# Projection of the second attention's last two chunks as entries of its score ring

## The reference

```python
x = x + _layernorm(_L0_attn_ref(_layernorm(x), ...))   # low-rank q and kv, rotary, causal softmax attention
x = x + _layernorm(_L0_ffn_ref(_layernorm(x), ...))    # int8 weights: silu(x Wg) * (x Wu), then Wd
x = x + _layernorm(_L1_attn_ref(_layernorm(x), ...))
x = x + _layernorm(_L1_ffn_ref(_layernorm(x), ...))
```

```python
qkv = jnp.einsum('bsd,ed->bse', x, w_qkv) + b_qkv
scores = jnp.einsum('bhqd,bhkd->bhqk', q, k) / math.sqrt(Hd) + causal
out = jnp.einsum('bhqk,bhkd->bhqd', jax.nn.softmax(scores), v)
return jnp.einsum('bsd,ed->bse', out, w_out) + b_out
```

## Time and profile before

| | us |
|---|---|
| median of 3 runs (1263.5 to 1268.62) | 1264.33 |
| profiled execution | 1264.68 |
| its span, first to last instruction | 1262.9 |
| TensorE busy | 1159.9 (92%) |
| VectorE busy | 1051.2 (83%) |
| ScalarE busy | 730.6 (58%) |
| GpSimd busy | 334.6 (26%) |

### The profile page before, as it was taken

One profiled execution on the slowest core, in us unless ns is written; L12 is line 12 of the kernel. 1 busy time (PEld: TensorE's weight loads), 2 busy tenths in 40 slices (PEclk: granted clock), 3 DMA queues, 4 the chain that ended last, 5 costly groups with the idle time before them and its releaser, 6 DMA issues.

```text
span 1262.9 us, 35540 instructions
## 1 busy us (share of the span) xinstructions
PE 1159.9 (92%) x14872; PEld 588.7 (47%) x14872; DVE 1051.2 (83%) x2746; ACT 730.6 (58%) x925; POOL 334.6 (26%) x561
## 2 busy tenths in 40 slices
PE   5779999999999998799997799999999999987996
PEld 4432344544444543565653324455444444454664
DVE  6869999999999863887776799999999988558776
ACT  2441377767677887244452507777767788843332
POOL 2321211122111223434342312111131112424443
PEclk9976699999999999899997759999999999998999
DMA  5263000211200000001123420021120000000001
GB/s 175 90 205 102 21 15 15 65 28 30 50 4 2 3 3 3 1 34 37 51 64 102 113 78 15 15 58 28 29 57 4 3 3 3 4 1 1 17 18 34
DMA packets 31600, 49.95 MB, mean 40 GB/s; under 512 B 7245, under 2 KB 24143, under 8 KB 31431
## 3 DMA queue, kind: packets, MB, share of 16 engines
q1 hardware_dynamic: 25376, 41.95, 11.9%
q0 software_dynamic: 5488, 5.34, 1.5%
q10 hardware_dynamic: 576, 0.39, 0.1%
HBM read 32.56 MB, written 14.68 MB: 37 GB/s over the span
## 4 chain that ended last, share of the span: by engine, by line
PE 69%; DVE 20%; issue 3%; POOL 2%; ACT 2%; DMA 2%; SPq 0%; ACTq 0%; POOLq 0%; DVEq 0%
PE ps L994 66%; DVE m_tile L874 6%; DVE ps L876 3%; DVE stats L717 2%; DVE region_p L730 2%; ACT region_p L645 1%; POOL q_stack L519 1%; PE ps L1169 1%; PE ps L989 1%; DVE k_stack L944 1%; DMA q_stack<-m_rows 1%; DVE region_p L754 1%; DMA q_parts<-parts 1%; DVE k_stack L941 1%; DVE region_p L843 1%
## 5 line engine op out<-in xcount | busy, mean ns | idle before, releaser
L645 ACT ACTIVATE region_p<-ps 128x1024 f32<-128x1024 f32 (+3 forms) x640 | 541.4, 894 | 243.3 <-PE ps L994 239.9
L874 DVE TENSOR_REDUCE m_tile<-ps 128x1 f32<-128x512 f32 x768 | 501.3, 685 | 32.6 <-PE ps L994 26.9
L994 PE MATMUL ps<-k_stack,q_stack 96*32 96x512 bf16 (+3 forms) x5120 | 434.0, 374 | 24.9 <-DVE m_tile L874 9.6
L994 PE MATMUL ps<-q_stack,k_stack 99*32 99x512 bf16 (+3 forms) x5120 | 351.3, 352 | 6.1 <-DMA q_stack<-m_rows 3.1
L994 PE MATMUL ps<-region_p,v_all 128*17 128x512 f32 (+3 forms) x2560 | 291.9, 528 | 5.3 <-POOL region_p L524 5.2
L876 DVE CUSTOM_DVE_ANT_0 ps<-ps,causal 128x128 f32<-128x128 f32 (+3 forms) x512 | 248.7, 497 | 33.6 <-PE ps L994 32.2
L994 PEld LDWEIGHTS ps<-k_stack,q_stack 96*32 96x32 bf16 x5120 | 144.5, 97 | 259.1 <-DVE m_tile L874 108.2
L994 PEld LDWEIGHTS ps<-q_stack,k_stack 99*32 99x32 bf16 x5120 | 141.3, 97 | 154.4 <-issue 58.3
L524 POOL TENSOR_SCALAR_AFFINE_SELECT region_p<-region_p 128x512 f32<-128x512 f32 x128 | 81.4, 637 | 276.9 <-ACT region_p L645 271.3
L994 PE MATMUL ps<-region_a,w_ffn 128*128 128x512 f16 x512 | 123.4, 386 | 5.2 <-DVE region_a L762 5.2
L679 ACT ACTIVATE k_stack<-ps,cols 128x512 f32<-128x512 f32 x64 | 44.1, 689 | 113.0 <-PE ps L994 112.8
(11 more groups left out here) (98 smaller groups left out, 881.9 us busy)
## 6 DMA issues: line engine op xcount, KB each, us to landing
k_parts<-parts SPq DMA_DIRECT2D x16, 384.0 KB, 2.9
q_parts<-parts SPq DMA_DIRECT2D x16, 384.0 KB, 2.7
q_stack<-q_parts SPq DMA_DIRECT2D x32, 192.0 KB
k_stack<-k_parts SPq DMA_DIRECT2D x32, 192.0 KB
q_stack<-q_parts SPq DMA_DIRECT2D x32, 128.0 KB
k_stack<-k_parts SPq DMA_DIRECT2D x32, 128.0 KB
X<-in_x SPq DMA_DIRECT2D x4, 512.0 KB, 6.8
q_stack<-q_parts SPq DMA_DIRECT2D x32, 64.0 KB
```

The lines of the kernel that those rows point to most:

```text
L645: nc.scalar.activation(probs[:, o.j % SLOTS, 2 * o.hp:2 * o.hp + 2, o.off:CH], psT[:, o.k % 2, :, o.off:CH], ACT.Exp, scale=SCALE).then_in ...
L874: nc.vector.tensor_reduce(maximum, scores, AX.X, ALU.max).then_inc(s.ring_free, 1)
L994: return pe.matmul(o, a, b, start=first, stop=last)
```

## The change

The second layer gets a turn string of its own, `TURNS_1`, with new kinds of turns beside S, M, T, V and Y. Three of them take a bank of the ring: x (a pair of transposes of the last chunk's activations), u (a unit, 8 to 15) and v (a value product, 4 to 7; capital V is still the probabilities' product). The others have no bank: r is the remainder of a unit on VectorE, m its middle part on ScalarE and low part on GpSimd, w the addition of the bias to a value product, b and e the normalization of the last chunk's residual.

Chunk 2 (units 8 to 11, values 4 and 5) leaves FFN 0, and chunks 2 and 3 are both projected inside the attention. The ring starts when FFN 0 is evacuated, with the u of unit 8 in front; the wait for the ones (`ones_in`) stands before the first T of group 1. Four buffers hold `x_chunk`: chunk 2 lies in `w_raw`, so the int8 weights of FFN 1 are loaded after chunk 2 has been read, and their cast is done in three pieces behind the output copies of steps 5, 6 and 7. SyncE loads chunk c of group 0 behind units 3, 7, 9 and 13, and all of group 1 right behind unit 13; units 14 and 15 are stored after that. Layer 0 keeps its order and its code.

```diff
+TURNS_1 = (
+    "uSSrbmuruvrwSSSSSSemuSvrwSSSSSSSxSSSSxSSSMSSSSSSSSSSSSSmmTSSSTSTSSTSVSSSTTSVSTSTuSruMrvSmmuwSvrw"
+    "TSSTSSSVSVSSSVSSTSTSSSSSSSSSSSSSSSSSSSSSSSSSSSSSSSSSSTSSVSTSTSSTSSSTSTSVSTSVSSTSTSVSSTMSSSTSTSSV"
+    "SSVSSTSSTSTSVSSTTSYSTSVSTSTSVSTSTSVSTSSTVSVSSTSTSSVSSTSTSSVSSTSTSVSSTSTSVSTMSTSSVSTSSTYSVSTSTSSV"
...
+SIDE_TURNS = {"x": "X", "u": "U", "v": "V", "b": "BRANCH", "e": "XHAT", "r": "REM", "w": "VALUE", "m": "MID"}
...
+    ORDERS = (ORDER, plan_attention(TURNS_1, EARLY, EARLY_V)[1])
...
-        x_chunk = region_p[:, NT * C:NT * C + 2 * KC * CH].rearrange("p (b k t) -> p b k t", b=2, k=KC)
+        x_chunk = [x.rearrange("p (k t) -> p k t", k=KC) for x in (
+            region_p[:, NT * C:NT * C + KC * CH], region_p[:, NT * C + KC * CH:NT * C + 2 * KC * CH],
+            w_raw[:].bitcast(F32)[:, 0:KC * CH], region_a[:, 3 * KC * CH:4 * KC * CH])]
+        A_LAST = region_a[:, 2 * KC * CH:3 * KC * CH].rearrange("p (i c) -> p i c", i=TPC)
...
-            return u // 4 if u % 4 == 3 else None
+            return u // 4 if u % 4 == (3 if u < EARLY else 1) else None
...
+        def ring_release(L, o):
+
+            if o.kind == "X":
+                return turn[2].moved_a, o.k + 1
+            if o.kind == "U":
+                return proj[1].rem, o.k + 1
+            if o.kind == "V":
+                return proj[1].v_sb, o.k + 1
+            return s.ring_free, L * RING_N + o.seq + 1
...
                     if c is not None:
                         parts_complete(chunk_units(L, c))
                         load_stacks(0, c)
+                        if L == 1 and c == NCH - 1:
+                            sp.wait_ge(ffn[0].down, NCH * NI)
+                            sp.wait_ge(s.t_filled, T_N + 1)
+                            for c1 in range(NCH):
+                                load_stacks(1, c1)
                 parts_complete(NU)
                 if L == 0:
                     sp.wait_ge(proj[L].v_ps, VU)
-                else:
-                    sp.wait_ge(ffn[0].down, NCH * NI)
-                sp.wait_ge(s.t_filled, L * T_N + 1)
-                for c in range(NCH):
-                    load_stacks(1, c)
+                    sp.wait_ge(s.t_filled, 1)
+                    for c in range(NCH):
+                        load_stacks(1, c)
                 for n, (g, Q) in enumerate(STEPS):
                     if g + 2 < NG:
...
-                for at, o in enumerate(ORDER):
-                    for u in LOW_AT.get(at, ()) if L == 1 else ():
-                        split_lo(1, u)
+                for at, o in enumerate(ORDERS[L]):
+                    if o.kind == "MID":
+                        split_lo(1, o.k)
+                    if L == 1 and at == CHUNK_2_READ:
+                        pool.wait_ge(proj[1].u_ps, 12)
+                        pool.wait_ge(proj[1].v_ps, 6)
+                        load_ffn(1)
                     if o.kind == "S" and o.last:
...
-                for u in range(EARLY * L, NU):
-                    for what, c in before(L, ACT_BEFORE, u):
-                        chunk_scalar(what, c)
-                    split_hi(L, u)
-                    if u > EARLY * L:
-                        split_mid(L, u - 1)
-                split_mid(L, NU - 1)
-                convert_ffn(L)
-
-                for o in ORDER:
+                if L == 0:
+                    for u in range(NU):
+                        for what, c in ACT_BEFORE.get(u, []):
+                            chunk_scalar(what, c)
+                        split_hi(0, u)
+                        if u > 0:
+                            split_mid(0, u - 1)
+                    split_mid(0, NU - 1)
+                    convert_ffn(0)
+
+                for o in ORDERS[L]:
+                    if o.kind == "XHAT":
+                        sqrt_residual(2, NCH - 1)
+                    if o.kind == "X":
+                        move_transposed(2, NCH - 1, (o.k % 2,))
+                    if o.kind == "U":
+                        split_hi(1, o.k)
+                    if o.kind == "MID":
...
+                        if L == 1 and 5 <= o.n < 8:
+                            convert_ffn(1, (o.n - 5,))
...
-                    if L == 1 and at in REM_AT:
-                        unit_rem(1, REM_AT[at])
-                    if L == 1 and at == VALUES_SB_AT:
-                        v_value(1, 6)
-                        v_value(1, 7)
+                for o in ORDERS[L]:
+                    if o.kind == "BRANCH":
+                        normalize_branch(2, NCH - 1)
+                        add_last(2)
+                        stats_residual(2, NCH - 1)
+                    if o.kind == "XHAT":
+                        normalize_residual(2, NCH - 1)
+                    if o.kind == "REM":
+                        unit_rem(1, o.k)
+                    if o.kind == "VALUE":
+                        v_value(1, o.k)
...
-                    side(0, "v", 4)
-                    side(0, "v", 5)
+                    pe.wait_ge(turn[2].moved_a, 6)
+                    pe.wait_ge(p.rem, EARLY)
+                    pe.wait_ge(p.v_sb, EARLY_V)
                     pe.wait_ge(f.evac, NT)
...
-                else:
-                    pe.wait_ge(ones_in, 48)
                 seen = set()
                 stepped = set()
-                for at, o in enumerate(ORDER):
-                    if L == 1 and at == X_AT:
-                        transpose_batch(2, NCH - 1)
-                    if L == 1 and at in UNITS_AT:
-                        unit_products(1, UNITS_AT[at])
-                    if L == 1 and at == VALUES_AT:
-                        v_products(1, 6)
-                        pe.wait_ge(p.rem, 14)
-                        v_products(1, 7)
-                    if L == 1 and at == FIRST_T:
-                        pe.wait_ge(p.rem, NU)
-                        pe.wait_ge(p.v_sb, VU)
+                valued = EARLY_V
+                for o in ORDERS[L]:
                     if o.ring is not None and o.ring >= RING:
-                        pe.wait_ge(s.ring_free, L * RING_N + o.ring - RING + 1)
+                        pe.wait_ge(*ring_release(L, IN_RING[L][o.ring - RING]))
+                    if o.kind == "X":
+                        transpose_pair(2, o.k)
+                    if o.kind == "U":
+                        unit_products(1, o.k)
+                    if o.kind == "V":
+                        v_products(1, o.k)
                     if o.kind == "S":
                         for c in (o.Q, o.c):
...
+                            if L == 1 and STEPS[o.n][0] == 1:
+                                pe.wait_ge(ones_in, 48)
...
+                        if L == 1 and o.kt // 2 >= valued:
+                            valued = o.kt // 2 + 1
+                            pe.wait_ge(p.v_sb, valued)
```

More of the change, by code:

```diff
@@ L103, in plan_attention @@
     order = []
-    ring = si = mt = yt = ti = pi = sel = 0
-    for turn in TURNS:
-        if turn == "S":
+    ring = si = mt = yt = ti = pi = sel = seq = 0
+    count = {"x": NT // 2 - 2, "u": early_units, "r": early_units, "m": early_units, "v": early_values, "w": early_values}
+    for turn in turns:
+        if turn in SIDE_TURNS:
+            order.append(Step(SIDE_TURNS[turn], k=count.get(turn), ring=ring if turn in "xuv" else None))
+            if turn in count:
+                count[turn] += 1
+        elif turn == "S":
             n, h, r, c = s_units[si]
@@ L109, in plan_attention @@
             last = si == len(s_units) or s_units[si][0] != n
-            order.append(Step("S", n, *steps[n], h=h, r=r, c=c, last=last, ring=ring))
+            order.append(Step("S", n, *steps[n], h=h, r=r, c=c, last=last, ring=ring, seq=seq))
         elif turn == "M":
-            order.append(Step("MT", mt, *steps[mt], ring=ring))
+            order.append(Step("MT", mt, *steps[mt], ring=ring, seq=seq))
             mt += 1
         elif turn == "Y":
-            order.append(Step("YT", yt, *steps[yt], ring=ring))
+            order.append(Step("YT", yt, *steps[yt], ring=ring, seq=seq))
             yt += 1
@@ L131, in plan_attention @@
                 pi += 1
-        ring += turn in "SMY"
+        ring += turn in "SMYxuv"
+        seq += turn in "SMY"
     assert (si, ti, pi) == (len(s_units), len(t_list), len(pv_list)) and mt == yt == len(steps)
@@ L137, in build_program @@
 def build_program(nc, D, out):
-    STEPS, ORDER = plan_attention()
+    NU, VU, EARLY, EARLY_V = 16, NT // 2, 8, 4
+    STEPS, ORDER = plan_attention(TURNS, NU, VU)
+    ORDERS = (ORDER, plan_attention(TURNS_1, EARLY, EARLY_V)[1])
     NSTEP = len(STEPS)
-    RING_N = sum(1 for o in ORDER if o.ring is not None)
+    RING_N = sum(1 for o in ORDER if o.seq is not None)
     T_N = sum(1 for o in ORDER if o.kind == "T")
@@ L569, in sqrt_residual, with move_transposed @@
                                      bias=eps[:]).then_inc(turn[k].std2, 1)
-            def move_transposed(k, b):
```

(7 more changed lines are left out.)

112 lines of the change are left out of this document (53 added, 59 removed).

## The result

The changed kernel takes 1288.0 us (1285.68 to 1290.52), the one before 1264.9 in the same comparison. The ratio of the comparison is 1.0173, 95% interval 1.0151 to 1.0194; the two medians divide to 1.018. The profiled execution is 1285.7 us.

What follows compares the result with a forecast made beforehand. TensorE was taken to bound the kernel (69% of the chain, VectorE 20%). Opening -6.0, stall +17.0, clock +2.5 and casts +3.7 on 1264.7 gave 1281.9, say 1282 us, range 1268 to 1292.

Steps and rivals of the forecast that it cites:

- main case: At attention 1's ninth step TensorE stalls 12 us or more; time 1274 to 1292 us, chance 0.70.
- decisive step: The last unit's late store holds up head group 2's loads in SyncE's in-order queue; TensorE stands still 17.0 us.
- The wait at the ninth step: TensorE's stall at the first score block needing head group 2: 5.8 + 22.5 - 11.3 = 17.0 us, bounds 8.3 and 25.4.
- The opening: Hand-over from FFN 0 to attention 1: earlier ring start, less work moved inside, gains 6 us; bounds 0 and 16.6.
- the case in which the idle time is filled: Rival, attention's first 60 us: spread units fill VectorE's idle 10.6 us, gain 16.6, time 1261.1; chance 0.12.
- The casts: Three FFN 1 weight casts behind steps 5, 6 and 7 delay exponentials, 3.7 us together; bounds 0 and 5.5.
- The clock: Low TensorE clock after the long idle stretch: 5 us at half speed, 2.5 lost; bounds 0 and 5.
- The pace of the repeated loads: Head group 2's query loads repeat their source, so stay slow even alone: 56 GB/s, 21.1 us for three.
- short stall: Rival at the ninth step: group 2 loads go at the keys' pace, TensorE waits 8.3 us, time 1271.7; chance 0.14.
- The sum: Whole kernel: 1264.7 - 6.0 + 17.0 + 2.5 + 3.7 = 1281.9, say 1282 us.

## Why the prediction was right

The time, 1288.0, lies in the range and 6 us above the value given. The main case came true, and its decisive step is shown twice over: taken out in two ways it gives 26 us back, and put alone into the kernel before it costs 20. The sizes were less good than the total: the wait was 6.7 us longer than given, and an opening 2.3 us better hid a part of that.

- **The wait at the ninth step** was sized 17.0 us and measured 23.7. Its parts: GpSimd's low part ended 2.3 us behind the middle part (871.08 to the store at 873.41) instead of 1.14, the store took 3.45 instead of 2.9, and the loads 26.8 instead of 22.5, together 6.0 us of the 6.7. The rest is TensorE's time: from the end of transposed block 112 (868.81 + 0.61 = 869.42) to its arrival at 879.97 it had 10.6 us, not 11.3. The rate of 56 GB/s for the queries was the right kind of row. Two things may have made the loads longer. The sum had the keys lying beside the queries, yet in two stretches of the wait about 3 of 16 engines were busy and it was a key load that came last; so late key pieces probably stood behind repeated queries on those few engines. And SyncE goes on: the loads of chunk 3 and of group 3's first queries were issued at 889.70 to 896.81, inside the wait. Engines in general were not short, since some 13 of 16 stood idle in these stretches. How the 4.3 us divide is argued, not tried.
- **The opening** was sized -6 and gave 8.3 at the end of step 4 (up to 14.7 at the end of step 1). The evacuation came at 664.65 where 663.4 was worked out. The fuller stretch from 684 to 715 speaks for a part of the case in which the idle time is filled, but the new order gave 6.4 us of the 14.7 back by step 4. That case did not decide, since the wait was twice the 12 us below which it would have.
- **The casts** were sized 3.7 and measured 4.6 by the steps, inside the bound of 5.5. The medians differ by 6.3, outside it, but 1.4 us of such a difference stands in the trace before the first cast.
- **The clock** was sized 2.5. The row from 904 to 909 has 0.57, the next 1.00; that is 5 us at about half speed, some 2 us. Of the two rows that the estimate named as low after idle time, the one at 745 is no such row: TensorE was busy for 4.70 of its 5 us.
- **The pace of the repeated loads** decided between 1282 and the short stall's 1271.7. It was weighed rightly: with spread loads the wait is 13.9, not 23.7. That this kernel's 1270.8 lies near the short stall's 1271.7 is chance: its wait is not 8.3, and some 6.5 us of its gain lie in the first attention.
- **The sum**, -8.3 + 23.7 + 2 + 4.6 = 22.0, stands against 21.0 between the two profiled executions. At step 8, where all four terms are in, the difference is 18.9, so the terms overstate it by 3.1 us, and step 9 brings 2.2 that no term has. The close agreement at the end is partly luck.

Without the wait the change is worth a little: 1261.9 against 1265.4. With its casts in gaps and spread loads it reaches 1250.3, of which the spread loads alone give 6.5 in the kernel before.

## What to carry to other kernels

When work moves into a later stage, follow the last piece of it past its own engine: the store, what queues behind that store, and who reads it. On an in-order DMA queue a store that nobody needs soon must not stand ahead of loads that someone does. And move the small jobs that go with it into gaps that the trace shows, not merely off the place where they stood.

## What was not expected of the hardware

A query load as three transfers, two of them with a repeated source, kept 0.12 to 0.18 of the DMA engines busy at 40 to 56 GB/s. As six transfers of 64 KB without repetition, with the key loads beside them, the loads ran at 197 GB/s with 0.96 busy, and twice the issues paid. The kernel before gained 6.5 us by it too, 5.5 of them by the end of the first step of attention 0. And one of four small loads issued into such a burst took 6.4 us to land where the median was 2.6; TensorE stood still for 2.1 us until about its landing.
